# Whole-image loads on two queues, the second pooled tile fifth, one resize block per output column, and a new instruction order

## The reference, cut to what matters

```python
x: (4, 128, 32, 32) float32
y = group_norm(x, 32 groups of 4 channels)
# the memory of y is read again as (B, H, W, C), so that 128 "channels" of a token are 128 neighbours in memory
g = window_attn(y, Wqkv, bqkv, scale) @ Wproj + bproj        # 2x2 windows, 8 heads of 16
l = y averaged over 2x2 pixels                               # then read again as (B, 16, 16, C)
l = window_attn(l, Wqkv, bqkv, scale)
l = resize(blur_rows(l) + blur_columns(l), (B, C, 32, 32), "bilinear")
out = x + transpose(g + l)
```

## Time and profile before

| | us |
|---|---|
| runs of before | 80.78, 80.90, 81.19, median 80.90 |
| the profiled execution: its own time | 80.81 |
| its span, first to last instruction | 79.1 |
| outside the span | 1.7 |
| PE busy | 70.1 of 79.1 |
| DVE, ACT, POOL busy | 58.6, 39.2, 54.3 |

### The profile page before, as it was taken

The page is one execution under the profiler, slowest core; times in us unless marked ns, Lnnn a source line. Parts: engine busy times, 40 slices in busy tenths (PEclk is TensorE's granted clock), DMA queues, the critical chain, the costliest instruction groups (busy, mean ns, idle before and its releaser), DMA issues.

```text
span 79.1 us, 1517 instructions
## 1 busy us (share of the span) xinstructions
PE 70.1 (89%) x524; PEld 53.8 (68%) x524; DVE 58.6 (74%) x89; ACT 39.2 (50%) x73; POOL 54.3 (69%) x79
## 2 busy tenths in 40 slices
PE   0994697999999999999999999999999999999500
PEld 0493497645655577684678657989599999899300
DVE  0015936899997997999799999999699998333600
ACT  0070030647967798666387675646365736370100
POOL 5917841990958258499899899999996619982000
PEclk9999999999999999999999999999999999999999
DMA  0899999100000000000000000000000000009385
GB/s 0 240 229 237 249 256 274 41 0 0 0 0 12 0 0 0 0 0 12 0 4 0 0 0 0 0 8 0 0 0 0 0 8 0 0 31 365 135 320 210
DMA packets 2375, 5.21 MB, mean 66 GB/s; under 512 B 832, under 2 KB 1088, under 8 KB 2368
## 3 DMA queue, kind: packets, MB, share of 16 engines
q1 hardware_dynamic: 1760, 3.74, 15.5%
q10 hardware_dynamic: 608, 1.38, 6.9%
HBM read 3.02 MB, written 2.10 MB: 65 GB/s over the span
## 4 chain that ended last, share of the span: by engine, by line
PE 81%; DMA 8%; DVE 2%; issue 1%; ACTq 1%; DVEq 1%
PE q_ps L756 12%; PE s_ps L795 9%; PE k_ps L747 9%; PE v_ps L773 8%; DMA x_sb<-in_x 8%; PE job_ps L831 7%; PE ot_ps L809 7%; PE job_ps L848 5%; PE job_ps L724 5%; PE q_ps L854 3%; PE v_ps L770 3%; PE k_ps L831 3%; PE k_ps L848 2%; PE v_ps L711 2%; PE s_ps L831 1%; PE v_ps L724 1%
## 5 line engine op out<-in xcount | busy, mean ns | idle before, releaser
L424 POOL TENSOR_TENSOR pv<-pv 128x512 f32<-128x512 f32 x18 | 22.9, 1273 | 3.8 <-DVE pv L658 3.3
L600 DVE TENSOR_TENSOR qk<-q_sb,k_ps 128x1536 f32<-128x1536 f32 x10 | 17.3, 1729 | 0.2 <-PE k_ps L747 0.2
L658 DVE TENSOR_TENSOR pv<-prob_w,v_ps 128x1536 f32<-128x1536 f32 x9 | 15.6, 1735 | 0.0
L557 DVE BATCH_NORM_STATS2 bn<-x_sb 128x6 f32<-128x512 f32 x8 | 5.4, 686 | 7.7 <-DMA x_sb<-in_x 7.7
L756 PE MATMUL q_ps<-xt,w_sb 128*128 128x512 f32 x16 | 9.2, 662 | 0.0
L535 ACT COPY ot<-ot_ps 128x512 f32<-128x512 f32 x9 | 5.3, 585 | 7.3 <-PE ot_ps L809 7.3
L498 ACT ACTIVATE q_sb<-q_ps,bias_qkv 128x512 f32<-128x512 f32 x10 | 6.8, 682 | 3.8 <-PE q_ps L756 3.6
L747 PE MATMUL k_ps<-xd,w_sb 128*128 128x384 f32 x20 | 8.6, 516 | 0.0
L773 PE MATMUL v_ps<-w_sb,xd 128*128 128x128 f32 x60 | 8.3, 275 | 0.0
L795 PE MATMUL s_ps<-qk,head_sum 128*32 128x192 f32 x160 | 7.5, 329 | 0.0
L773 PEld LDWEIGHTS v_ps<-w_sb,xd 128*128 128x128 f32 x60 | 7.5, 192 | 0.0
(11 more groups left out here) (92 smaller groups left out, 127.3 us busy)
## 6 DMA issues: line engine op xcount, KB each, us to landing
out<-out_sb SPq DMA_DIRECT2D x3, 512.0 KB, 2.6
x_sb<-in_x SPq DMA_DIRECT2D x4, 256.0 KB, 6.9
x_sb<-in_x ACTq DMA_DIRECT2D x4, 256.0 KB, 7.3
resize_sb<-in_resize SPq DMA_DIRECT2D x1, 640.0 KB, 8.8
out<-out_sb SPq DMA_DIRECT2D x1, 256.0 KB, 3.4
out<-out_sb ACTq DMA_DIRECT2D x1, 256.0 KB, 3.5
w_sb<-in_L_conv_Wqkv SPq DMA_DIRECT2D x1, 192.0 KB, 7.6
wp_sb<-in_L_conv_Wproj ACTq DMA_DIRECT2D x1, 64.0 KB, 9.6
```

The source lines that it names most:

```text
L424: nc.gpsimd.tensor_tensor(first, first, other, ALU.add).then_inc(summed[i], 1)
L600: nc.vector.tensor_tensor(qk[:, m % 2, :, :, n % 2, :], q, k, ALU.mult).then_inc(qk_done, 1)
L658: nc.vector.tensor_tensor(to, p, v, ALU.mult).then_inc(pv_done, 1)
```

## The change

Eight things change together:

1. SP loads images 0 and 2 whole (128 partitions, 512 KB), ACT images 1 and 3 whole. The QKV weights stand on SP between images 0 and 2, the projection weights move to SP's queue behind the biases.
2. The pooled tile (None, 1) becomes tile 5 and (2, 0) tile 6.
3. The resize matrix has eight blocks in place of ten. Four new copies on ACT per pair of images ("mid") put the two half columns that groups 3 and 4 need into `middle`; "low" runs four matmuls in place of five, and waits for `middle_out`.
4. ("xt", 0, 1) writes into k_ps[1] in place of job_ps.
5. DVE's "diff" (tiles 0 and 1) takes tokens 1 to 3 from the PSUM bank of the transpose in place of `xt`.
6. The last pair's denominators on DVE are one reduction in place of two additions.
7. The warm-up matmuls have the same column count in the first place and one block fewer in the last, in five wide instructions of the code in place of eleven narrow ones; ("zero",) goes behind ("K", 0).
8. The order on every engine and the order of stores.

```diff
-TILES = [(0, 0), (0, 1), (1, 0), (None, 0), (1, 1), (2, 0), (None, 1), (2, 1), (3, 0), (3, 1)]
+TILES = [(0, 0), (0, 1), (1, 0), (None, 0), (1, 1), (None, 1), (2, 0), (2, 1), (3, 0), (3, 1)]
...
+        block = np.concatenate([r[1, :64, k], r[0, 64:, k]]) if part == 2 else r[part, :, k]
...
 "PE": [
-        ("mean", 0), ("var", 0), ("mean", 1), ("var", 1), ("xt", 0, 0), ("xt", 0, 1), ("zero",), ("Q", 0), ("K", 0),
-        ("xt", 1, 0), ("Q", 1), ("mean", 2), ("lt", 0), ("K", 1), ("Q", 2), ("var", 2), ("xt", 1, 1), ("K", 2),
+        ("mean", 0), ("var", 0), ("mean", 1), ("var", 1), ("xt", 0, 0), ("xt", 0, 1), ("Q", 0), ("K", 0), ("zero",),
+        ("xt", 1, 0), ("Q", 1), ("mean", 2), ("lt", 0), ("K", 1), ("var", 2), ("Q", 2), ("xt", 1, 1), ("K", 2),
...
-        ("S", 3), ("O", 3), ("V", 6), ("low", 0, 0), ("K", 9), ("out", 0, 0), ("O", 4), ("V", 7), ("low", 1, 1),
-        ("out", 1, 1), ("S", 4), ("O", 5), ("low", 0, 1), ("V", 8), ("out", 0, 1), ("V", 9), ("O", 6),
-        ("low", 1, 0), ("low", 3, 0), ("O", 7), ("low", 2, 1), ("low", 3, 1), ("out", 2, 1), ("O", 8), ("O", 9, 0),
-        ("out", 1, 0), ("out", 3, 0), ("O", 9, 2), ("low", 2, 0), ("O", 9, 1), ("out", 3, 1, 0), ("O", 9, 3),
-        ("out", 2, 0), ("out", 3, 1, 1),
+        ("Q", 9), ("S", 3), ("O", 3), ("V", 6), ("K", 9), ("low", 0, 0), ("out", 0, 0), ("O", 4), ("V", 7),
+        ("low", 1, 0), ("out", 1, 0), ("S", 4), ("O", 5), ("low", 0, 1), ("V", 8), ("out", 0, 1), ("O", 6),
+        ("V", 9), ("low", 1, 1), ("low", 2, 1), ("O", 7), ("out", 1, 1), ("low", 3, 1), ("out", 2, 1),
+        ("low", 2, 0), ("O", 9, 0), ("O", 8), ("out", 2, 0), ("O", 9, 2), ("low", 3, 0), ("O", 9, 1),
+        ("out", 3, 1, 0), ("O", 9, 3), ("out", 3, 0), ("out", 3, 1, 1),
...
 "ACT": [
+        ("Qo", 8), ("Oo", 2), ("Vo", 5), ("sd", 3), ("Oo", 3), ("mid", 0), ("E", 3), ("Qo", 9), ("sd", 4),
+        ("Vo", 6), ("res", 0, 0), ("Oo", 4), ("Vo", 7), ("sd", 5), ("res", 1, 0), ("Oo", 5), ("E", 4), ("sd", 6),
+        ("mid", 1), ("res", 0, 1), ("Vo", 8), ("Oo", 6), ("Vo", 9), ("sd", 7), ("Oo", 7), ("res", 1, 1), ("sd", 8),
...
 "DVE": [
         ("bn", 0, 0), ("bn", 0, 1), ("bn", 1, 0), ("dev", 0), ("bn", 1, 1), ("gvar", 0), ("bn", 2, 0), ("dev", 1),
-        ("scale", 0, 0), ("gvar", 1), ("scale", 0, 1), ("bn", 3, 0), ("diff", 0), ("bn", 3, 1), ("diff", 1),
-        ("bn", 2, 1), ("M", 0), ("dev", 2), ("M", 1), ("gvar", 2), ("M", 2), ("X", 0), ("M", 3), ("R", 0), ("M", 4),
+        ("scale", 0, 0), ("gvar", 1), ("scale", 0, 1), ("bn", 2, 1), ("diff", 0), ("bn", 3, 0), ("diff", 1),
+        ("bn", 3, 1), ("dev", 2), ("M", 0), ("gvar", 2), ("M", 1), ("M", 2), ("X", 0), ("M", 3), ("R", 0), ("M", 4),
...
-        ("P", 9, 3), ("res", 2, 1), ("res", 3, 0, 1), ("res", 3, 0, 0), ("res", 3, 1, None, 0), ("res", 2, 0),
-        ("res", 3, 1, 0, 1), ("res", 3, 1, 1, 1),
+        ("res", 2, 1), ("P", 9, 3), ("res", 2, 0), ("res", 3, 1, None, 0), ("res", 3, 0, 0), ("res", 3, 1, 0, 1),
+        ("res", 3, 1, 1, 1), ("res", 3, 0, 1),
...
-WARM = {("mean", 0): 5, ("var", 0): 1, ("mean", 1): 5}
-STORES = [0, 1, 2]
+WARM = {("mean", 0): (4, 2), ("var", 0): (1,), ("mean", 1): (2, 2)}
+STORES = [0, 2, 1]
...
+            if job == ("xt", 0, 1):
+                return k_ps[1]
...
-            for b in range(2):
-                sp.dma_start(x_sb[0:64, b, :], x_chan[b, 0:64]).then_inc(x_loaded[b], 16)
-            sp.dma_start(w_sb[:, :], w_qkv).then_inc(w_loaded, 16)
-            for b in range(2, B):
-                sp.dma_start(x_sb[0:64, b, :], x_chan[b, 0:64]).then_inc(x_loaded[b], 16)
+            for b in (0, 2):
+                sp.dma_start(x_sb[:, b, :], x_chan[b]).then_inc(x_loaded[b], 16)
+                if b == 0:
+                    sp.dma_start(w_sb[:, :], w_qkv).then_inc(w_loaded, 16)
...
+            sp.dma_start(wp_sb[:, :], w_proj).then_inc(wp_loaded, 16)
...
-            for b in range(B):
-                act.dma_start(x_sb[64:128, b, :], x_chan[b, 64:128]).then_inc(x_loaded[b], 16)
-            act.dma_start(wp_sb[:, :], w_proj).then_inc(wp_loaded, 16)
+            for b in (1, 3):
+                act.dma_start(x_sb[:, b, :], x_chan[b]).then_inc(x_loaded[b], 16)
...
+            def middle_part(p):
+
+                low = TILES.index((None, p))
+                act.wait_ge(ot_out, low + 1)
+                parts = ot[:, low, :].rearrange("f (e h i a x) -> f i h a e x", e=2, h=2, i=2, a=8)
+                for half in range(2):
+                    at = slice(64 * half, 64 * (half + 1))
+                    for i in range(2):
+                        ins = nc.scalar.copy(middle[at, p, i, :].rearrange("f (a e x) -> f a e x", a=8, e=2),
+                                             parts[at, i, 1 - half])
+                    ins.then_inc(middle_out, 1)
...
-                less_token_0(nc.vector, n).then_inc(diff_dve, 1)
+                less_token_0(nc.vector, n, bank(("xt", *TILES[n]))).then_inc(diff_dve, 1)
...
+                    nc.vector.tensor_reduce(denom[:, m % 2, :], by_window(expd[:, m % 2, :]), AX.X,
                                             ALU.add).then_inc(denom_done, 1)
...
+                pe.wait_ge(middle_out, 2 * nth("ACT", ("mid", b // 2)))
...
-            def keep_warm(n):
-                for _ in range(n):
-                    nc.tensor.matmul(q_ps[:, 0:P], ident[:, :], ident[:, :], start=True, stop=True)
+            def keep_warm(*columns):
+                for n in columns:
+                    nc.tensor.matmul(q_ps[:, 0:n * P], ident[:, :], ident[:, :].unsqueeze(1).broadcast_to([P, n, P]),
+                                     start=True, stop=True)
```

More of the change, by code:

```diff
@@ L67, in resize_blocks @@
     r = r.T.reshape(KL, P, K, P)
-    used = [(k, l) for k in range(K) for l in range(KL) if r[l, :, k].any()]
-    return used, np.stack([r[l, :, k] for k, l in used], 1).astype(np.float32)
-BLOCKS, RESIZE = resize_blocks()
+    blocks = []
+    for k in range(K):
+        part = 2 if k in MIDDLE else k // WIN
+        block = np.concatenate([r[1, :64, k], r[0, 64:, k]]) if part == 2 else r[part, :, k]
+        assert np.abs(block).sum() == np.abs(r[:, :, k]).sum()
+        blocks.append((part, block))
+    return [part for part, _ in blocks], np.stack([block for _, block in blocks], 1).astype(np.float32)
+PARTS, RESIZE = resize_blocks()
 ORDER = {
     "PE": [
-        ("mean", 0), ("var", 0), ("mean", 1), ("var", 1), ("xt", 0, 0), ("xt", 0, 1), ("zero",), ("Q", 0), ("K", 0),
[6 rows of a table removed]
-        ("low", 1, 0), ("low", 3, 0), ("O", 7), ("low", 2, 1), ("low", 3, 1), ("out", 2, 1), ("O", 8), ("O", 9, 0),
-        ("out", 1, 0), ("out", 3, 0), ("O", 9, 2), ("low", 2, 0), ("O", 9, 1), ("out", 3, 1, 0), ("O", 9, 3),
-        ("out", 2, 0), ("out", 3, 1, 1),
+        ("mean", 0), ("var", 0), ("mean", 1), ("var", 1), ("xt", 0, 0), ("xt", 0, 1), ("Q", 0), ("K", 0), ("zero",),
[6 rows of a table added]
+        ("V", 9), ("low", 1, 1), ("low", 2, 1), ("O", 7), ("out", 1, 1), ("low", 3, 1), ("out", 2, 1),
+        ("low", 2, 0), ("O", 9, 0), ("O", 8), ("out", 2, 0), ("O", 9, 2), ("low", 3, 0), ("O", 9, 1),
+        ("out", 3, 1, 0), ("O", 9, 3), ("out", 3, 0), ("out", 3, 1, 1),
     ],
@@ L99 @@
         ("low", 0), ("xto", 0, 0), ("xto", 0, 1), ("scale", 1, 0), ("Qo", 0), ("low", 1), ("xto", 1, 0), ("Qo", 1),
-        ("lto", 0), ("scale", 1, 1), ("Qo", 2), ("xto", 1, 1), ("Qo", 3), ("scale", 2, 0), ("low", 2), ("E", 0),
-        ("low", 3), ("Qo", 4), ("xto", 2, 0), ("scale", 3, 0), ("scale", 2, 1), ("lto", 1), ("scale", 3, 1),
[6 rows of a table removed]
+        ("lto", 0), ("scale", 1, 1), ("Qo", 2), ("xto", 1, 1), ("low", 3), ("Qo", 3), ("low", 2), ("scale", 2, 0),
[7 rows of a table added]
     ],
@@ L195, in conv_attention_kernel @@
         ot = sb("ot", [P, N, 512])
+        middle = sb("middle", [P, PAIRS, 2, P])
         out_sb = sb("out_sb", [P, B, PIX])
@@ L306, in tokens, with less_token_0 @@
             return xl[:, k, :] if b is None else xt[:, b, k, :]
-        def less_token_0(engine, n):
+        def less_token_0(engine, n, turned=None):
             x = tokens(n).rearrange("f (j w) -> f j w", j=WIN)
-            return engine.tensor_tensor(xd[:, n, :].rearrange("f (j w) -> f j w", j=KEYS), x[:, 1:],
+            others = x if turned is None else turned[:, :].rearrange("f (j w) -> f j w", j=WIN)
+            return engine.tensor_tensor(xd[:, n, :].rearrange("f (j w) -> f j w", j=KEYS), others[:, 1:],
                                         x[:, 0:1].broadcast_to([P, KEYS, NW]), ALU.subtract)
@@ L549, in _ @@
                  "Qo": queries_out, "Vo": values_out, "sd": value_0_put, "E": exponent,
-                 "Oo": attention_out, "res": result}[kind](*at)
+                 "Oo": attention_out, "mid": middle_part, "res": result}[kind](*at)
             last_half(act, 1)
@@ L687, in bank_free @@
                 earlier = [j for j in earlier[:earlier.index(job)] if bank(j) is bank(job)]
-                if earlier:
```

(18 more changed lines are left out.)

26 lines of the change are left out of this document (12 added, 14 removed), and 26 rows, old and new, of the table ORDER.

## The result

| | before | after |
|---|---|---|
| median of four runs on one chip, us | 80.84 | 77.26 |
| lowest to highest, us | 80.72 to 81.19 | 77.08 to 78.81 |
| the profiled execution, us | 80.81 | 77.08 |
| its span, us | 79.1 | 75.4 |

The ratio is 0.954, with a 95% interval of 0.950 to 0.9585: 4.6% faster. The forecast was 77.3 us.

What follows compares the result with a forecast made beforehand. PE was taken as the bound: when its run of work starts, its length and pace, and what follows. From 80.81 us, -1.3 + 0.3 - 1.8 + 0.4 - 1.1 = -3.5 gave 77.3 us, range 75.8 to 79.8.

Steps and rivals of the forecast that it cites:

- The loads: Image loads at launch: 350 GB/s in place of 244, images 0, 1 and 2 landed at 5.3, 7.1 and 9.4 us.
- The start: PE's work up to "dev" 1: it runs at 11.05 in place of 12.33, gaining 1.3 us.
- PE's pace: Early PE work: more of it runs at half pace before the clock rises, costing 0.3 us, at most 0.65.
- DVE and POOL at the start: Cheaper differences (some 0.56 us each) and "dev" 2 before M 0 change nothing on PE: 0, bound 0.5 us.
- Resize blocks: "low" on PE: 64 instructions for 80 gain 1.8 us; waiting for ACT's "mid" 0 copies loses 0.4.
- The last pair: Last denominators on DVE: D 4 comes 1.05 us earlier, gaining nothing itself; without it O 8 up to 1 us late.
- The middle: The rearranged order from 20 to 50 us: no term in the sum, possible waits left to rival B.
- rival B: The new order starves PE, above all at mid 0 or S 0, store gain half used: about 79.3 us, chance 0.15.
- The end: Last stores: only image 3's halves come last, landing 2.2 us after issue in place of 3.5, gaining 1.1 us.
- Rival A: Image loads stay near 244 GB/s, image 2 lands at 13.0 and the start loses 1.35: 79.7 us, chance 0.15.
- C: Slower than before: image 2 arrives so late that "dev" 1 eats all other gains: 82.0 us, chance 0.07.
- D: Nothing gained: PE's savings are all given back to waits for POOL and DVE: 80.9 us, chance 0.05.

Runs made afterwards that it cites:

- the two experiments on loads: Half-image loads put back in the changed kernel: 78.24 us, ratio 0.9736; whole-image loads alone put into the kernel before: 79.95 us, ratio 0.9926.
- the one queue: The changed kernel with all four whole images on SP's queue, in order, weights behind image 1: 75.07 us, ratio 0.9178 to the kernel before.
- the control: The changed kernel, unaltered, profiled and timed again: 77.21 us, ratio 0.9597 to the kernel before.
- the moved wait: The changed kernel with PE waiting for middle only before the matmul that reads it, placed last of its part: 77.10 us.
- the late image 2: The changed kernel with DVE's last result of image 2 put behind image 3's first two: 80.33 us, ratio 0.9987 to the kernel before.

## Why the prediction was right, point by point

**What bounds the kernel** held: the chain is 78% PE, and what moved the time was the start of its run, its length, and what follows it.

**The loads.** Rate 350 forecast, 414 measured. The step that mattered, that whole-image loads to 128 partitions escape the 244 GB/s, is shown from both sides by the two experiments on loads. By the Trainium skill, SBUF — State Buffer, "Door 1: The DMA port swizzle", partitions 0 to 63 reach half of the ports, and 247 against 414 GB/s at equal share agrees with that. Arrival was forecast at 5.3, 7.1 and 9.4; the images landed at 5.5, 5.7 and 8.8 and were used at 5.47, 6.92 and 9.19, the last two without a wait. Image 0 gained nothing although the rate rose by 70%, as image 1 shares the engines meanwhile; the one queue shows the price, 1.37 us. By the Trainium skill, DMA: Bandwidth & Descriptors, "Issuing engines are not separate DMA queues", the queues interleave, and the landings of images 0 and 1, 0.2 us apart, agree with that. The forecast let SP's queue have the first 0.9 us alone and used that rule for the range only. Its 5.3 was nearly met because the rate was higher than assumed, and its 7.1 for image 1 only because DVE is not free for that image before 6.9: luck in both.

**The start** was put at -1.3. "dev" 1 came 1.14 us earlier (11.19, forecast 11.05; the warm-up runs to 10.94, forecast 10.8). It hangs on the pace of the four warm-up blocks: over the eight profiles named next "dev" 1 stands at 10.00 to 11.30, in the control at 10.91.

**PE's pace** was put at +0.3, with 0.65 if the clock rises at the same moment of the launch as before. To the end of S 0 the first profile gained 1.71 in all, 0.57 more than "dev" 1 did; in the control "dev" 1 comes 1.42 us earlier and S 0 ends 1.49 earlier, a surplus of 0.07. Over eight profiles of seven kernels with whole images on two queues and the same warm-up, PE doing the same up to S 0, S 0 ended at 23.83, 23.85, 23.95, 23.97, 24.07, 24.18, 25.09 and 25.30. The last two (the moved wait and the late image 2) are the ones that can be laid beside the profile of the kernel before, as all three have a granted clock of 1.00 all through the start and the slow pair at Q 0. Their "dev" 1 comes 1.03 and 1.15 earlier than before, their S 0 only 0.47 and 0.26: against its like the pace takes 0.6 to 0.9 us back, the sign that was forecast. There is one profile only of the kernel before, so how often its clock rises earlier is not known. This term is the least certain of the sum.

**DVE and POOL at the start** at 0: the differences took 0.56 us each as estimated, and taking them back changed nothing.

**Resize blocks.** -1.8 forecast; 64 instructions are there, 0.89 us for eight, and 1.34 of the 1.8 is measured directly by the ten blocks put back. The other 0.45 lies between S 3 and S 4. The wait for "mid" 0 was put at +0.4 and is 0.43; the four copies took 1.0 us as estimated.

**The last pair** was right in its sum, 0, and wrong in its reason: "without it O 8 would be late by up to 1 us" fell. With the two additions S 4 to PE's end took 15.59 in place of 15.54.

**The middle** is where a term was missing. S 2 to S 3 lost 0.71 with the same items on PE. Reading the two timelines of DVE: before, P 3 ended 5.94 us after S 2's end; after, 6.65. The rows of the kernel before, P 3 and R 2, to be laid beside the chain of the kernel after, where `inv` is in front:

```profile
42.56 1.75 DVE L658 TENSOR_TENSOR pv<-prob_w,v_ps 128x1536 f32<-128x1536 f32 x1
44.23 0.54 DVE L621 RECIPROCAL inv<-denom 128x64 f32<-128x64 f32 x1
```

In front of P 3 now stands R 2, 0.46 from its start to the next, and P 2 starts 1.16 in place of 0.87 us after S 2, because ("xt", 3, 1) is now in front of O 0 on PE, and P 2 may not write its products before O 0 has read the ones in the same buffer. 0.46 + 0.29 = 0.75. V 5 waits for P 3. That is argued from the timelines; of tests, the tile order is excluded, and R 2 put back alone brings P 3 forward by 0.4 but makes the stretch longer through POOL. ("xt", 3, 1) was not moved alone, nor DVE's and POOL's places together. The forecast left the middle at nothing in its sum and gave it to rival B.

**The end.** -1.1 forecast, -1.27 measured: the last store lands 2.1 us after its issue (2.2 forecast, 3.5 before), and is issued 1.07 us after PE's end in place of 0.91. The reason, no other store in front of image 3's, is borne out by the moved result, which cost 3 us, more than the term; as that edit also holds back image 1's store and puts 0.6 us of DVE's work behind PE, it does not measure image 2's store alone.

**In sum**: start and pace -1.71 (forecast -1.0), S 0 to S 3 +0.76 (0), S 3 to S 4 -0.04 and S 4 to PE's end -1.44 (together -1.4), tail -1.27 (-1.1): -3.7 against -3.5. The start's surplus and the missed term of the middle, both 0.7, cancelled. That the total came out within 0.1 us is luck, owed to this: with an S 0 at 25.09 or 25.30 the same sum gives -2.5 or -2.25. That it came out under before, and by the loads, the blocks and the stores, is owed to the mechanisms. Rival A (244 GB/s) and C (image 2 late) fell with the 414 GB/s; B was right in one wait of 0.7 and wrong in size; D fell. B's own sum, 77.3 + 0.5 + 1.1 and half of the store gain, is 79.45 and not 79.3. The store order alone, the bank of xt (0, 1), the place of ("zero",) and the weights' queues were not tried by themselves.

## What to carry to other kernels

- Load to all 128 partitions at once, and ask of each transfer what shares the engines with it until it lands: the one that is waited for first should run alone, even at a lower total rate (a mean of 311 GB/s and image 0 1.4 us earlier, against 414).
- At the end, count what is still to leave when the last result is ready, and whether a store that is ready stands behind one that isn't on the same queue: one result moved by two places cost 3 us, more than the sixteen matmul instructions that the change removes are worth (1.8).
- When an order is rewritten on several engines, compare each stretch between two fixed pieces of work, not the total. A wait of 0.7 us and a gain of 0.7 us can hide in a total that fits. Where a stretch does not repeat between profiles, as the one up to S 0 here, one profile per kernel does not say what an edit did to it.
